# A graph network layer on one core: the segment sums of groups 0 to 5 made in steps 82 to 87, the nodes' x part in steps 89 to 95

## The reference

```python
edge_in = concatenate([h[row], h[col], dist], axis=1)       # row = src, col = dst, dist = edge_weight1
e = silu(edge_in @ eW1 + eb1)                               # 129 -> 128
e = silu(e @ eW2 + eb2)                                     # 128 -> 128
agg = segment_sum(e, row, num_segments=3125)
node_in = concatenate([h, agg], axis=1)
out = silu(node_in @ nW1 + nb1) @ nW2 + nb2                 # 192 -> 128 -> 64
return layernorm(x + out)                                   # over the 64 features
```

## Time and profile before

| | |
|---|---|
| median of 3 runs | 631.85 us |
| span of the profiled execution, first to last instruction | 629.0 us |
| median less span | 2.85 us |
| busy: PE / PE weight loads | 530.9 / 447.6 us |
| busy: DVE / ACT / POOL | 463.5 / 355.5 / 429.0 us |
| granted clock of PE, mean | 0.962 |
| indirect row loads on POOL | 440, first at 39.3, last at 607.4 us |

### The profile page before, as it was taken

How to read it: one execution, slowest core, us unless ns; L and a number is a source line. 1 busy time by engine, 2 the same in 40 slices (tenths; PEclk the granted TensorE clock), 3 DMA queues, 4 the chain that set the end, 5 groups by cost and what they waited for, 6 DMA issues and landing times.

```text
span 629.0 us, 15166 instructions
## 1 busy us (share of the span) xinstructions
PE 530.9 (84%) x4653; PEld 447.6 (71%) x4653; DVE 463.5 (74%) x1364; ACT 355.5 (57%) x812; POOL 429.0 (68%) x465
## 2 busy tenths in 40 slices
PE   4942869879879989998998899889997888879795
PEld 3421658768768869887887778778776777769684
DVE  6987999988999899989888869797642533223356
ACT  5842555455555556755655555565556666656464
POOL 2337576566777777777777777777777777777750
PEclk9986899779999999999999999999999999999997
DMA  5211111111111121111121111111111121111111
GB/s 121 77 51 51 43 52 48 36 50 48 56 52 52 52 56 56 52 56 49 54 56 52 51 55 56 53 52 55 54 54 55 52 56 54 53 55 53 55 39 51
DMA packets 17215, 34.17 MB, mean 54 GB/s; under 512 B 8133, under 2 KB 9352, under 8 KB 17142
## 3 DMA queue, kind: packets, MB, share of 16 engines
q0 software_dynamic: 14080, 28.86, 16.0%
q1 hardware_dynamic: 2594, 3.40, 2.1%
q10 hardware_dynamic: 468, 0.96, 0.6%
HBM read 30.73 MB, written 2.40 MB: 53 GB/s over the span
## 4 chain that ended last, share of the span: by engine, by line
POOL 32%; DVE 25%; PE 21%; issue 16%; DMA 3%; DVEq 1%; SPq 0%; POOLq 0%
POOL q_rows L736 32%; PE layer_ps L749 9%; PE sort_ps L749 6%; PE seg_ps L749 5%; DVE load_hot L1212 3%; DVE agg L1283 3%; DVE count L1058 2%; DMA q_rows<-q_table,q_index 2%; DVE hot L1268 2%; DVE col_hot L1206 1%; DVE row_hot L1207 1%; DVE place L1102 1%; PE turn_ps L841 1%; DMA src_i<-in_src_dram 1%; DVE slot L1108 1%
## 5 line engine op out<-in xcount | busy, mean ns | idle before, releaser
L736 POOL DMA_INDIRECT q_rows<-q_table,q_index x440 | 419.4, 953 | 159.5 <-issue 127.6
L583 ACT ACTIVATE e<-layer_ps 128x512 f32<-128x512 f32 x110 | 65.7, 597 | 212.7 <-PE seg_ps L749 204.3
L1283 DVE TENSOR_TENSOR agg<-agg,seg_ps 128x125 f32 x416 | 93.3, 281 | 93.5 <-PE seg_ps L749 90.3
L749 PE MATMUL layer_ps<-hotT,p_table 128*128 128x128 bf16 x1320 | 158.8, 225 | 0.2
L749 PE MATMUL layer_ps<-ident_f,q_rows 128*128 128x128 f32 x440 | 126.7, 288 | 33.6 <-DMA q_rows<-q_table,q_index 32.8
L749 PE MATMUL seg_ps<-hot,e 128*128 128x125 f32 x880 | 125.1, 286 | 23.9 <-DVE agg L1283 23.9
L749 PEld LDWEIGHTS layer_ps<-hotT,p_table 128*128 x1320 | 122.3, 98 | 22.7 <-issue 2.3
L749 PEld LDWEIGHTS seg_ps<-hot,e 128*128 128x128 f32 x880 | 109.5, 196 | 27.3 <-issue 25.3
L749 PE MATMUL layer_ps<-w_sb,h 128*128 128x128 f32 x880 | 119.5, 279 | 0.0
L749 PEld LDWEIGHTS layer_ps<-w_sb,h 128*128 128x128 f32 x880 | 111.2, 193 | 4.6 <-issue 0.2
L749 PEld LDWEIGHTS layer_ps<-ident_f,q_rows 128*128 128x128 f32 x440 | 63.0, 143 | 44.3 <-DMA q_rows<-q_table,q_index 43.3
(11 more groups left out here) (193 smaller groups left out, 439.9 us busy)
## 6 DMA issues: line engine op xcount, KB each, us to landing
q_rows<-q_table,q_index POOLq DMA_INDIRECT x440
q_table<-q_in_sb SPq DMA_DIRECT2D x1, 784.0 KB
x_sb<-in_x_dram ACTq DMA_DIRECT2D x1, 700.0 KB
q_table<-q_in_sb SPq DMA_DIRECT2D x1, 616.0 KB
out_dram<-x_sb SPq DMA_DIRECT2D x2, 224.0 KB
out_dram<-x_sb SPq DMA_DIRECT2D x1, 252.0 KB
w_in<-in_edge_weight_dram SPq DMA_DIRECT2D x1, 185.9 KB
dst_i<-in_dst_dram SPq DMA_DIRECT2D x1, 185.9 KB
```

The costliest lines, as they stand in the source:

```text
L583: A.activation(e2[:, m % 2, :], e_of(m)[:], ACT.Silu).then_inc(e2_ready, 1)
L736: P.indirect_dma_start(q_rows[:, g % RING, j, :], None, q_table, bass.IndirectOffsetOnAxis(ap=q_index[:, GT * g + j:GT * g + j + 1], axis= ...
L749: return nc.tensor.matmul(o, lhsT, rhs, start=start, stop=stop, **kw)
L1283: D.tensor_tensor(o, o, seg_ps[:, j * LO:(j + 1) * LO], ALU.add).then_inc(agg_added, 1)
```

## The change

The segment sums of groups 0 to 5 are not made in steps 4 to 9. Their second silu goes to memory of its own, `e2_kept`, which is the first part of `q_in_sb`, and their float32 one-hots to `hot32_kept`. PE makes the six sums in steps 82 to 87, between `second_layer` and `first_layer`, with a signal `kept_ready`, and DVE adds them in the same steps behind the add of the running group. Since sums are no longer in order of m, the count of adds that a sum or an add waits for is looked up in `ADDED_BEFORE`. The node parts go from steps 84, 86, ... 96 to steps 89 to 95, and ACT's copy of them waits for the six kept sums. `squared` moves into the memory of `hot32_kept`.

```diff
+KEPT = 6
+KEPT_STEP = 82
+SEGMENTED = list(range(KEPT, KEPT_STEP - 4))
+for d in range(KEPT):
+    SEGMENTED += [d, KEPT_STEP - 4 + d]
+SEGMENTED += range(KEPT_STEP - 4 + KEPT, GROUPS)
+ADDED_BEFORE = {m: GT * n for n, m in enumerate(SEGMENTED)}
...
     for n in range(7):
-        at(TENSOR, 84 + 2 * n, (NODE_X, n, 0))
+        at(TENSOR, KEPT_STEP + KEPT + 1 + n, (NODE_X, n, 0))
...
+        hot32_kept_sb = sb("hot32_kept", [128, KEPT * GT * LO])
+        e2_kept = q_in_sb[:, 0:KEPT * GT * 128].rearrange("p (d f) -> p d f", d=KEPT)
...
             def convert(g):
-                if g >= 4:
+                if g >= KEPT + 4:
                     act.wait_ge(*seg_done(g - 4))
-                A.activation(hot32[:, g % 4], hot[:, g % HOT_RING, :, 0:LO], ACT.Copy).then_inc(hot32_ready, 1)
+                A.activation(hot32_of(g), hot[:, g % HOT_RING, :, 0:LO], ACT.Copy).then_inc(hot32_ready, 1)
...
             def silu2(m):
                 act.wait_ge(*second_done(m))
-                if m >= 2:
+                if m == 0:
+                    act.wait_ge(q_stored, 64)
+                if m >= KEPT + 2:
                     act.wait_ge(*seg_done(m - 2))
-                A.activation(e2[:, m % 2, :], e_of(m)[:], ACT.Silu).then_inc(e2_ready, 1)
+                A.activation(e2_of(m), e_of(m)[:], ACT.Silu).then_inc(e2_ready, 1)
...
             def node_x(n):
-                act.wait_ge(q_stored, 64)
+                act.wait_ge(kept_ready, KEPT)
...
             def segment(m):
-                if m >= 1:
-                    pe.wait_ge(agg_added, m * GT)
+                if ADDED_BEFORE[m]:
+                    pe.wait_ge(agg_added, ADDED_BEFORE[m])
...
                 if 2 <= m <= TIGHT:
                     second_layer(m - 2)
+                if KEPT_STEP <= m < KEPT_STEP + KEPT:
+                    segment(m - KEPT_STEP).then_inc(kept_ready, 1)
                 first = first_layer(m)
...
-                if 4 <= m <= TIGHT:
+                if KEPT + 4 <= m <= TIGHT:
                     last = segment(m - 4)
...
-                    dve.wait_ge(*seg_done(m))
+                    if m < KEPT:
+                        dve.wait_ge(kept_ready, m + 1)
+                    else:
+                        dve.wait_ge(*seg_done(m))
...
-                if 5 <= m <= TIGHT:
+                if KEPT + 5 <= m <= TIGHT:
                     add_segments(m - 5)
+                if KEPT_STEP <= m < KEPT_STEP + KEPT:
+                    add_segments(m - KEPT_STEP)
```

More of the change, by code:

```diff
@@ L101 @@
 HOT_STEP = [-1] * len(batches(0))
+KEPT = 6
[5 more added lines that the diff above has]
+ADDED_BEFORE = {m: GT * n for n, m in enumerate(SEGMENTED)}
+assert len(ADDED_BEFORE) == GROUPS
 def plan():
@@ L321, in build @@
         hot32 = sb("hot32", [128, 4, GT, LO])
+        hot32_kept_sb = sb("hot32_kept", [128, KEPT * GT * LO])
+        hot32_kept = hot32_kept_sb[:].rearrange("p (d j l) -> p d j l", d=KEPT, j=GT)
         hotT = sb("hotT", [128, TURNED, GT * 128], BF16)
@@ L329, in build @@
         square = sb("square", [LO, NF])
-        squared = sb("squared", [LO, 1 + len(ACT_SQUARES), GT, NF])
+        squared = hot32_kept_sb[0:LO, 0:(1 + len(ACT_SQUARES)) * GT * NF].rearrange("p (n b f) -> p n b f", b=GT, f=NF)
         stat = sb("stat", [LO, 4, WIN])
@@ L380, in build @@
                  "to_ready hots_ready sort_mm sorted_ready index_ready sort_read w_split w_full w_parted "
-                 "hot_ready w_placed hotT_ps_ready hotT_ready hot32_ready step_ready pre_ready h1_ready e_ready e2_ready seg_ready "
+                 "hot_ready w_placed hotT_ps_ready hotT_ready hot32_ready step_ready pre_ready h1_ready e_ready e2_ready seg_ready kept_ready "
                  "agg_added agg_whole hx_ps_ready hx_ready x_centred hid_ps_ready hid_summed hid_ready y_ready y_read ln_var ln_squared ln_squares ln_sd ln_done ln_inverse ln_first out_stored").split()
@@ L387, in build @@
          to_ready, hots_ready, sort_mm, sorted_ready, index_ready, sort_read, w_split, w_full, w_parted,
-         hot_ready, w_placed, hotT_ps_ready, hotT_ready, hot32_ready, step_ready, pre_ready, h1_ready, e_ready, e2_ready, seg_ready,
+         hot_ready, w_placed, hotT_ps_ready, hotT_ready, hot32_ready, step_ready, pre_ready, h1_ready, e_ready, e2_ready, seg_ready, kept_ready,
          agg_added, agg_whole, hx_ps_ready, hx_ready, x_centred, hid_ps_ready, hid_summed, hid_ready, y_ready, y_read, ln_var, ln_squared, ln_squares, ln_sd, ln_done, ln_inverse, ln_first, out_stored) = (
@@ L405, in seg_done, with hot32_of, e2_of @@
             return (step_ready, m + 5) if m < TIGHT - 3 else (seg_ready, m - TIGHT + 4)
+        def hot32_of(g):
+            return hot32_kept[:, g] if g < KEPT else hot32[:, g % 4]
+        def e2_of(m):
+            return e2_kept[:, m] if m < KEPT else e2[:, m % 2]
         def turn_done(g):
@@ L878, in segment @@
                 pe.wait_ge(hot32_ready, m + 1)
-                if m >= 1:
-                    pe.wait_ge(agg_added, m * GT)
+                if ADDED_BEFORE[m]:
+                    pe.wait_ge(agg_added, ADDED_BEFORE[m])
                 for j in range(GT):
-                    last = mm(seg_ps[:, j * LO:(j + 1) * LO], e2[:, m % 2, j * HID:(j + 1) * HID],
-                              hot32[:, m % 4, j, :], True, True)
+                    last = mm(seg_ps[:, j * LO:(j + 1) * LO], e2_of(m)[:, j * HID:(j + 1) * HID],
+                              hot32_of(m)[:, j, :], True, True)
                 return last
@@ L1277, in add_segments @@
                         skip_runtime_bounds_check_because="a window's number is a count of 24 comparisons")[1]
-                    dve.wait_ge(*seg_done(m))
+                    if m < KEPT:
+                        dve.wait_ge(kept_ready, m + 1)
+                    else:
+                        dve.wait_ge(*seg_done(m))
                     for j in range(GT):
-                        if m * GT + j >= 2:
-                            dve.wait_ge(agg_added, m * GT + j - 1)
+                        if ADDED_BEFORE[m] + j >= 2:
+                            dve.wait_ge(agg_added, ADDED_BEFORE[m] + j - 1)
                         o = agg[j % 2][:, bass.ds(windows[j], LO)]
```

## The result

The changed kernel takes 625.05 us (median of 4 runs, 624.29 to 626.41) against 631.88 us: a ratio of 0.9906, interval 0.9886 to 0.9926. In a second set with more runs it is 625.91 us, 0.9898 (0.9869 to 0.9928). The forecast was 628.15 us and its range ended at 626.0. The direction was right, the gain is 5.9 to 6.8 us where 3.7 were forecast.

What follows compares the result with a forecast made beforehand. POOL's indirect row loads bound the kernel, 5.0 us a group, held up by PE and DVE until 196 us. 631.85 - 3.7 (early steps) + 0 (late steps) = 628.15 us; range 626 to 631.2.

Steps and rivals of the forecast that it cites:

- Where the time is: Up to 196 us POOL is late by PE and DVE, then runs 5.0 us a group; earlier gains shift everything after.
- The chain from 84 to 105 us: Steps 6 to 8, without early sums and adds: close of chunk 2 at 104.5 instead of 108.32 us, gain 3.8 us.
- All that follows is relative to this point.: POOL's issue of group 14 comes at 117.9 instead of 121.56 us; the stalls at 137.7 to 195.8 remain.
- The unchanged low-clock stretch in step 10: PE's 1.04 + 4.01 + 0.43 + 1.40 us to 121.29 stay at the low clock, after a longer idle.
- rival C: Low-clock stretch 114.41 to 121.29 us ends sooner, 2.7 us less: 6.4 us gained, 625.5 us; chance 0.14.
- The late steps at no cost: Steps 82 to 95: six PE sums of 0.95 us and 24 DVE adds of 0.22 us cost 0, bounds 0 and +1 us.
- The base: The 2.85 us between the profiled span of 629.0 us and the median carry over unchanged; span after 625.3 us.
- The signs that I had named: Wrong if POOL's issue of group 14 shifts under 2 or over 5 us, or POOL waits for PE after 460 us.

Runs made afterwards that it cites:

- node_only: The kernel before with only the node parts moved, to steps 89 to 95 instead of 84 to 96 by twos: 631.07 us, 0.9987.
- again: The changed kernel once more, unchanged: 625.91 us.
- no_late_sums: The changed kernel with the six sums of groups 0 to 5 and their adds in steps 82 to 87 left out: 625.69 us, 0.9903.
- before_1: The kernel before, unchanged, traced a second time: 628.79 us, one execution.
- before_2: The kernel before, unchanged, traced a third time: 632.78 us, one execution.
- filler_step9: The changed kernel with eleven more matmuls of 512 columns on PE in step 9, ahead of OFFSET of chunk 3: 625.63 us, 0.9911.
- dve_only: The kernel before with DVE's adds of groups 0 to 5 left out, PE's segment sums all where they were: 628.85 us, 0.9953.
- pe_only: The kernel before with PE's segment sums of groups 0 to 5 left out, DVE's adds all where they were: 630.13 us, 0.9981.

## Why the prediction was too small, point by point

**Where the time is.** Right. POOL isn't stalled after 196 us, and what PE and DVE gain before arrives whole. Means over the four traces with the schedule of before (node_only among them) and the three of the changed one: 106.5 to 101.9 us from group 9 to 28 is 4.6 us; 412.0 to 411.0 us after it, 0.9 us, which I had not forecast.

**The chain from 84 to 105 us.** Right to 0.3 us in the first trace, too small in the others. Counted from group 9's issue, the close was to be at 104.5 - 88.94 = 15.6 us and is at 105.23 - 89.43 = 15.8; in again and no_late_sums it is at 15.1 and 14.5. It scatters in the kernel before as well: 19.4 in the trace that I read, 17.9 and 20.5 in before_1 and before_2. The clock was low for batch 1 and for half of the layers (3.21 instead of 2.02 us), as I took it. What I had not seen is a low stretch at 88 to 91 us, after the idle of 2.5 us in step 5; it costs nothing, because DVE is later than PE there.

**"All that follows is relative to this point."** This step failed. I had released group 14, at 121.56, as the point that sets the rest, on PE's path, and took 3.7 us from it. filler_step9 moved that point by 1.6 to 2.2 us more and group 17 stayed. What sets group 17 is step 13's segment sum, which waits until DVE has added group 8. DVE comes to that add by one queue that starts with READ (in the first trace after it waits for PE once in it, 0.32 us). Both traces of the rows above, counted from group 9's issue: READ begins at 19.5 us before and at 15.9 after, 3.6 us sooner, which is the term I had; from READ to the start of the sum it takes 26.97 us before and 26.39 after, 0.6 us less, since the add of group 5 stood behind READ and is gone; the sum itself takes 1.75 instead of 2.04 us. That makes 3.6 + 0.6 + 0.3 = 4.5 us at group 17. In again and no_late_sums READ is 4.3 and 4.8 us sooner than in that trace of before, and group 17 5.1 us. The sentence that DVE's products come earlier by 0.8 us a block was in the prediction, and I didn't follow it past the close. It isn't DVE's path alone: ahead of READ DVE waits for PE, 1.83 us in the first trace and 0.58 in the two others. dve_only brings 3.5 us and pe_only 1.35.

**How much of the miss that is.** The forecast was 3.1 us too slow. Span to span, the first two traces lie 4.5 us apart: so 0.8 us belong to the stages, and the other 2.3 us to the base, below. The 4.5 us are 4.7 up to group 28 and 0.35 behind it, less 0.5 by which group 9 itself came later. What belongs to the base is not a mechanism but the luck of the trace.

**The unchanged low-clock stretch in step 10.** Wrong as a fact: it ended near 115 us, after 3.7 instead of 6.3, which was rival C. It was worth nothing at group 17, which C did not see either. Nor did the change shorten it: before_1 and before_2 have the low clock here only from 115.1 to 118.5 and from 116.5 to 119.9 us. The long stretch belongs to two of the four traces of that schedule, the first and node_only (114.2 to 121.0 us).

**The late steps at no cost.** Right by no_late_sums, 0.2 us. The small numbers were off: PE waited 0.28 us for DVE's add before five of the kept sums, and 1.49 us before one, with the residual ahead of that add (forecast 0.2 at most). POOL saw neither.

**The base.** I carried 2.85 us between span and median over unchanged. The executions of both kernels have 1.8 to 2.4 us around their span (1.8 to 1.9 in 17 of the kernel before), so the trace of before, with its span of 629.0 us, will have been an execution of about 630.9 us (an estimate: its own time isn't on record), 1 us below the median, and the trace after was one 1.4 us above its own. That is the difference between 4.5 us (span to span) and 6.8 us (median to median).

**The signs that I had named.** They would have let the prediction pass: the issue of group 14 came 4.5 us sooner, within 2 to 5, and POOL never waited for PE in the late steps beyond its 0.30 us. A sign can be met and the mechanism behind it be another.

**What stays open.** 4.6 + 0.9 = 5.5 us are found in the stages, less 0.3 us by which group 9 itself comes later in the traces of the changed kernel (89.2 and 89.5 us in the means), where the change can't reach it. The medians lie 5.9 to 6.8 us apart. Three or four traces of each kernel don't fix the means closer than that.

## What to carry to other kernels

When work is taken from two engines at once, follow each engine's own queue to the next place where the bound engine is released, and not only to the first: a release that comes sooner is worth nothing if the one behind it is set by another engine. Here that was 0.6 us of 4.5. Filler work in a wait is a cheap test of whether a low clock behind it counts: in step 9 it moved one release and no more, in step 13 it gained 2 us. Take a second and third trace before a forecast of a per cent or less; here one kernel's stage differed by 2.5 us between traces.

## What the runs showed of the hardware

PE's clock falls at places that differ from execution to execution of one kernel, after the same idle time. In step 5 PE is idle for 1.28 and then 0.88 us in before_1 and in before_2 alike; behind it the granted clock is 0.50 in the one and 1.00 in the other, which then loses it behind an idle of 3.06 us in step 6. So a single trace doesn't tell which idle stretch costs the clock. What a low stretch costs is a matter of what waits behind it: 0.2 us at group 10 in the one, 1.8 us in the other.

After group 28 some of POOL's issues take 1.1 to 2.2 us instead of 0.94, none to three in a chunk. Each of them runs beside an instruction of DVE with both inputs in SBUF, most beside the two products `place<-place,in_win`. One in before_2:

```profile
282.63 0.41 DVE L1133 TENSOR_SCALAR dest_hot<-iota_f,dest_col 100x408 bf16<-100x408 f32 x1
282.69 2.02 POOL L736 DMA_INDIRECT q_rows<-q_table,q_index  x1 [0.30 <-issue]
282.98 0.51 DVE L1106 TENSOR_TENSOR place<-place,in_win 125x351 f32<-125x351 f32 x1
283.41 0.48 DVE L1107 TENSOR_TENSOR place<-place,in_win 125x324 f32<-125x324 f32 x1
```

POOL's issue ends 0.82 us after the second product. Where DVE's instruction begins only 0.9 us into the issue, the issue takes 1.12 to 1.16 us. In the other cases it ends 0.8 us after such an instruction of DVE: after the only one or the first of two (1.12 to 1.45 us in all), or after the second (1.6 to 2.2 us). So a shift of the whole schedule changes the sum of long issues, 2.2 to 4.1 us in the traces of the kernel before and 1.9 to 2.3 us in those of the changed one. That is the 0.9 us after group 28, by coincidence and not by design. The table bears it out: less its long issues, that stage takes 408.5 to 408.8 us in every run but the changed kernel's first trace, where it is 409.35.

Neither the products nor `dest_hot` are needed for it. Near the end of the first trace of before an issue is long beside the sum of the two copies of `agg`, which has both inputs in SBUF too:

```profile
604.34 0.68 DVE L1297 TENSOR_TENSOR agg<-agg 128x500 f32<-128x500 f32 x1
604.37 1.45 POOL L736 DMA_INDIRECT q_rows<-q_table,q_index  x1 [0.30 <-issue]
```

The Trainium skill (SBUF — State Buffer, Who interferes with whom) says that a DVE instruction with two inputs in SBUF contends with a GpSimd instruction that reads SBUF. The trace agrees: the products and this sum have two such inputs, and the issues take 2.02 and 1.45 us against 0.94. The same section infers that such an instruction would not hold up the writing of descriptors; for indirect loads these rows show otherwise, and the measurement decides. The adds, with one input in PSUM, leave POOL at 3.78 us in 5.00, which is the rule's other half. The overlap was seen and not tested by taking the products away.
